# Global attention on one core: the values of two units back move ahead of the pair of trial scores

## What is computed

```python
def _L1_attn_ref(x, Wq, Wk, Wv, Wu, bu):      # b=2, t=1024, e=64, h=8
    scale = e ** (-0.25)
    q = (x @ Wq).reshape(b, t, h, e) * scale
    k = (x @ Wk).reshape(b, t, h, e) * scale
    v = (x @ Wv).reshape(b, t, h, e)
    dot = jnp.einsum('bqhe,bkhe->bhqk', q, k)
    att = jax.nn.softmax(dot, axis=-1)
    out = jnp.einsum('bhqk,bkhe->bqhe', att, v).reshape(b, t, h * e)
    return out @ Wu + bu
```

## Time and profile before

| | us |
|---|---|
| runs of the kernel before, three | 602.72, 610.61, 612.91 |
| their median | 610.61 |
| the profiled execution, device time | 602.83 |
| its span | 600.8 |
| PE busy in the span | 529.1 (88%) |
| DVE busy | 404.9 (67%) |
| ACT busy | 318.4 (53%) |
| global attention, from the first scores at 169.14 to about 476 | about 307 |

### The profile page before, as it was taken

The page is one execution under the profiler, slowest core; times in us unless marked ns, Lnnn a source line. Parts: engine busy times, 40 slices in busy tenths (PEclk is TensorE's granted clock), DMA queues, the critical chain, the costliest instruction groups (busy, mean ns, idle before and its releaser), DMA issues.

```text
span 600.8 us, 10365 instructions
## 1 busy us (share of the span) xinstructions
PE 529.1 (88%) x3951; PEld 255.0 (42%) x3952; DVE 404.9 (67%) x740; ACT 318.4 (53%) x584; POOL 49.8 (8%) x106
## 2 busy tenths in 40 slices
PE   6999998998599989999999999999999652799962
PEld 5554654554133335444334443344444320366721
DVE  5655557357886746876887686876662556898662
ACT  2735445565256575556656566666656332655440
POOL 7031232113110000000000010000000000000000
PEclk9999999699679999999999999999999957999975
DMA  5000000000000000000000000000000000000001
GB/s 112 5 1 2 2 2 2 0 2 2 0 1 1 1 1 1 2 0 1 1 1 1 1 2 1 1 9 1 1 1 1 2 3 15 1 1 1 1 0 35
DMA packets 9511, 3.28 MB, mean 5 GB/s; under 512 B 8820, under 2 KB 9079, under 8 KB 9463
## 3 DMA queue, kind: packets, MB, share of 16 engines
q1 hardware_dynamic: 8182, 2.61, 1.9%
q10 hardware_dynamic: 1281, 0.01, 0.1%
HBM read 2.09 MB, written 0.52 MB: 4 GB/s over the span
## 4 chain that ended last, share of the span: by engine, by line
PE 76%; DVE 10%; issue 8%; ACT 3%; POOL 1%; POOLq 0%; DVEq 0%; ACTq 0%
PE PS L786 18%; PE PS L763 18%; PE PS L747 5%; PE PS L667 4%; PE PS L681 4%; PE PS L694 3%; PE PS L518 2%; PE PS L490 2%; PE PS L502 2%; PE PS L802 2%; PE PS L708 2%; PE PS L989 2%; PE PS L564 2%; DVE most L1550 2%; PE PS L582 1%
## 5 line engine op out<-in xcount | busy, mean ns | idle before, releaser
L1189 ACT ACTIVATE PT<-PS 128x512 f32<-128x512 f32 x256 | 138.7, 593 | 78.7 <-PE PS L763 78.3
L1550 DVE TENSOR_REDUCE most<-PS 128x2 f32<-128x1024 f32 x128 | 154.4, 1221 | 33.9 <-PE PS L747 33.0
L763 PE MATMUL PS<-qrow,aS 128*64 128x512 f16 x1024 | 134.5, 383 | 1.8 <-ACT PT L1189 1.8
L786 PE MATMUL PS<-PT,V 128*64 128x512 f32 x512 | 134.4, 604 | 0.0
L763 PEld LDWEIGHTS PS<-qrow,aS 128*64 128x64 f16 x1024 | 58.8, 110 | 68.8 <-issue 22.9
L1145 ACT ACTIVATE prob<-sbias,negm 128x320 f32<-128x320 f32 (+1 forms) x64 | 34.3, 537 | 44.1 <-DVE negm L1596 43.9
L747 PE MATMUL PS<-aS,qrow 64*128 64x512 f16 x256 | 41.6, 397 | 7.0 <-DVE most L1550 6.2
L786 PEld LDWEIGHTS PS<-PT,V 128*64 128x64 f32 x512 | 32.0, 136 | 37.0 <-ACT PT L1189 17.9
L667 PE MATMUL PS<-ident 128*128 128x256 f16 x128 | 39.1, 306 | 7.5 <-DVE negm L1596 6.3
L1307 POOL TENSOR_TENSOR rstd<-var,minus_half 128x8 f32<-128x8 f32 (+1 forms) x9 | 13.5, 1505 | 343.5 <-DVE var L1414 343.5
L339 DVE COPY PT<-PS 128x384 f32<-128x384 f32 (+1 forms) x32 | 16.7, 523 | 29.4 <-PE PS L694 29.3
(11 more groups left out here) (192 smaller groups left out, 657.2 us busy)
## 6 DMA issues: line engine op xcount, KB each, us to landing
xall<-in_x_dram SPq DMA_DIRECT2D x2, 256.0 KB, 4.4
out_dram<-x SPq DMA_DIRECT2D x4, 128.0 KB, 2.1
w<-in_L_attn_Wq_dram SPq DMA_DIRECT2D x2, 128.0 KB, 2.6
w<-in_L_attn_Wk_dram SPq DMA_DIRECT2D x2, 128.0 KB, 2.7
w<-in_L_attn_Wv_dram SPq DMA_DIRECT2D x2, 128.0 KB, 2.7
fc<-in_L_conv_fc_w_dram SPq DMA_DIRECT2D x2, 64.0 KB, 2.7
wu<-in_L_attn_Wu_dram SPq DMA_DIRECT2D x2, 64.0 KB, 2.3
w1s<-in_L_ffn_ffn_w_dram SPq DMA_DIRECT2D x2, 64.0 KB, 2.1
```

What stands on the lines that cost most here:

```text
L763: mm = pe.matmul(PS[h0:h0 + C, lane, :], aS[:, part, k0 + h0:k0 + h0 + C], qG[:, lane, toks], start=(part == 0), stop=(part == 1))
L786: mm = pe.matmul(PS[cols, 6 + g % 2, :], V[:, img * NT + kt, cols], PT[:, g % 2, lane, kt, :], start=(kt == 0), stop=(kt == NT - 1))
L1189: act.activation(PT[:, g % 2, lane, phase, :], PS[:, lane, :], ACT.Exp).then_inc(c1["exped"], 1)
L1550: dve.tensor_reduce(most[:, g % 2, u // 2, u % 2, :], PS[:, b0:b0 + 2, :], AX.X, ALU.max, negate=True)\
```

## The change

Within a step of the global attention's loop the call of `glob_values(t - LAG_VAL)` stands ahead of the two calls of `try_scores` instead of behind them. Nothing else is changed: the same instructions, the same waits, the same banks.

```diff
                 if 0 <= t < UNITS:
                     scores(t)
+                if 0 <= t - LAG_VAL < UNITS:
+                    glob_values(t - LAG_VAL)
                 if 0 <= t + AHEAD < UNITS and (t + AHEAD) % 2 == 0:
                     try_scores(t + AHEAD)
                     try_scores(t + AHEAD + 1)
-                if 0 <= t - LAG_VAL < UNITS:
-                    glob_values(t - LAG_VAL)
                 if 1 <= g <= NG and phase in (Y_PHASE, Y_PHASE + 1):
                     head_outputs(g - 1, phase - Y_PHASE)
```

## The result

The changed kernel is slower. Its median was 618.34 us (609.08 to 620.44, 4 runs) beside 606.66 us for the kernel before, a ratio of 1.0174 (95% interval 1.0104 to 1.0244). The ratios leave out the executions that took over 1.5% more than the fastest of their kernel (here 620.44 and the profiled 619.74), so they are not the quotients of the medians. The two intervals only just meet, so the whole time alone gives the loss no better than "0.3 to 2.4%". The traces give it closer, once the stretch before the change is set aside.

A forecast was written before the change was run, and what follows sets the result against it. PE was taken as the bound of the global attention, with DVE setting the end at L816's wait; 9.1 - 1.3 + 0.7 = +8.5 us on 602.83 gave 611.3, or 619.1 from the median, put at 614, range 603 to 621.

The forecast's parts named there:

- The bound and the wait: Global attention: PE's list sets the time, except where L816 in phase 6 waits for DVE's second low query.
- Term 1: Phase 5: later trials delay DVE's reduction and low query, so L816 comes 0.70 us later; +9.1 us over 13 groups.
- Values followed by trials, 0.96: PE's blocks in changed steps: values to trials take 0.96 us start to start, bounds 0.86 and 1.01.
- Term 2: The 44 other changed steps: PE's blocks take 2.38 us instead of 2.41, -1.3 us in all.
- Term 3: L725 in phase 4 waits for L1666: 0 in quiet groups, +0.7 us in group 6 behind the key table.
- Sum: Whole kernel: 9.1 - 1.3 + 0.7 = +8.5 us.
- A: L816's wait is for something the trials don't move; 602.2 us, chance 0.12.
- B: PE's blocks fit better, values to trials 0.86 and trials to scores 0.43; 600 us, chance 0.06.
- C: L725 in phase 4 waits in all groups 1 to 12, adding 8.8 us; 620 us, chance 0.10.
- D: Longer PE gaps before L816 in groups 3 and 9 drop the granted clock; 616 us, chance 0.04.

The follow-up runs named there:

- e9: Kernel before, with one 0.69 us addition put on DVE's list ahead of phase 5's first reduction; ratio 1.0114, quiet group 18.95 us against 18.35.
- e2: Kernel before, with values ahead of trials in all phases but phase 5; quiet group 18.29 us against 18.35, no ratio given.
- e11: The changed kernel measured again on another chip with more rounds; 610.43 us beside 604.33 for the kernel before, ratio 1.0073.
- e10: Kernel before, with values first except in phase 5, second low query earlier, additions in phase 6, key table one step earlier; 597.43 us beside 604.33, ratio 0.9869.
- e7: Kernel before, with DVE's second low query right behind phase 5's first reduction and output additions moved to phase 6; ratio 0.9911, quiet group 18.07 us.

## Why the prediction was right, point by point

**The bound and the wait.** PE's list is the bound and L816's wait for the second low query is the one real wait of a quiet group: e9 lengthens that wait alone and pays in full.

**Term 1.** The trials stand 1.82 behind the scores, the reduction 2.25, L816 5.09, each as worked out. In groups 0 to 12 the way from the scores to L816 grew by 9.05 in all; the forecast was 13 x 0.70 = +9.1. Right, mechanism and size.

**Values followed by trials, 0.96.** Taken from L582's row. Measured 336.06 to 337.02: 0.96. Trials followed by scores 0.54 as well.

**Term 2.** Forecast -0.03 for a changed step, measured -0.06 for three steps in e2, so -0.02. Too small to matter. But I left out what follows the pair in some steps, and three of them count most. In steps 9, 15 and 17 a product L582 follows, and that one has the shape of the trials. These are the rows of step 15 in the changed kernel:

```profile
214.83 1.06 PE L763 MATMUL PS<-qrow,aS 128*64 128x512 f16 x8
215.69 1.05 PE L786 MATMUL PS<-PT,V 128*64 128x512 f32 x4
216.67 0.60 PE L747 MATMUL PS<-aS,qrow 64*128 64x512 f16 x4
217.12 1.02 PE L582 MATMUL PS<-prob,fc 64*128 64x512 f32 x2
218.06 1.05 PE L763 MATMUL PS<-qrow,aS 128*64 128x512 f16 x8
```

Scores to scores is 3.23 here and was 3.58 before (204.80 to 208.38). Trials to L582 is 0.45, where a change of shape behind trials makes it 0.54, and the values no longer stand between two changes of shape. Another 0.11 lies behind L582: 0.94 to the next scores here, 1.05 before (207.33 to 208.38), and why is open. This is the sum's mistake: three times -0.35, about -1 us. It is why group 2 (steps 15 and 17) was no longer than before, 23.87 against 23.86, in spite of its +0.70 at L816. Five more steps (7, 23, 39, 79 and 87) have L555, L591, L825 or L830 behind the pair; they became 0.14 to 0.24 shorter where the other steps of phase 7 became 0.05 shorter, which is another 0.6 us. The rule of the Trainium skill that I weighed (TensorEngine Tiling (Array Packing), Key Properties) says that a change of tiling mode drains the array. I had counted two changes in every step for either order. That holds where scores follow; with L582 behind the pair the old order has four changes up to the next scores and the new one two, at about 0.10 each. The rule agrees with these rows as far as those 0.20 of the 0.35 go; my count didn't.

**Term 3.** L725 held its place in quiet groups: its margin of 0.1 was enough. In group 6 the forecast was +0.7 on top; the group got 1.35 longer where quiet ones got 0.64. Right.

**Sum.** +8.5 forecast, +7.4 in e11's trace. The three L582 steps are about -1.0 of the difference and the five others -0.7; the remaining 36 steps of term 2 gave 0.02 each and not 0.03, +0.4. Terms 1 and 3 came out as forecast.

**The rivals.** A is out (L816 waits in all 13 groups). B is out: 0.96 and 0.54, not 0.86 and 0.43; a small part of it was true in the three steps. C is out: L725 waits in no quiet group. D is out: the granted clock is 1.00 in every window from 200 to 470 us, across gaps of up to 1.43 us in front of L816.

**The time.** 618.34 against a forecast of 614, within 603 to 621. That it lies so near to 614 is in part luck (609.6, where the runs of e11 gather, would have been in the range too): the change cost less than forecast, and three of the four runs had a mean granted clock of only 0.918 to 0.929, where the sum started from an execution at 0.942. I had put the time between two levels seen in three runs. The 17 runs of the kernel before beside e10 and e11 show something less tidy: eight lie at 602.3 to 603.1 with a mean granted clock of 0.942 to 0.945, three at 604.3 to 606.7, and six at 608.0 to 617.5 with 0.928 to 0.915. The sum was for the first kind; four of the changed kernel's twelve runs in e11 lie at 609.5 to 609.7, also at 0.945 to 0.948, 7.0 above. The forecast for an execution like the profiled one, 611.3, was 1.7 too high.

## What to carry to other kernels

Moving a block on the bounding engine costs nothing there and yet can cost a lot: ask for each consumer of the block what stands behind it in the consumer's in-order list, and whether the bounding engine waits for that later on. A mean busy share doesn't answer this; DVE was idle 30% of the time and had no slack at the one place. Where the result has several consumers with different slack, the order can be chosen per place (here: trials first in phase 5, values first elsewhere), and the dependent work that is urgent should stand ahead of what is not (the low query ahead of the additions): that was worth 0.9% (e7), and 1.3% with the order chosen per place and the key table a step earlier (e10). And count changes of the array's tile shape with the neighbour that really follows, not with the usual one.

## What the runs showed of the hardware that was not expected

With identical instructions the first 156 us ran at mean granted clocks of 0.90 to 0.98, and the first scores started anywhere from 168.1 to 177.4 us. That is more than the change is worth, and may be why two ratios of the same kernel are 1.0174 and 1.0073. What sets it was not tried and stays open, and the mean clock of the first 156 us doesn't tell it all: at 0.95 the first scores came at 168.14 in e2 and at 173.60 in e11.

A change of tile shape showed as 0.10 us at each border (scores to trials 0.97 instead of 0.86, values to trials 0.96), and was absent between two blocks of the same shape (trials to L582 0.45 against 0.54 to scores or outputs). The listed shape isn't all of it: L825 is a transpose listed as 128*64 like the values, and yet in the kernel before values behind trials took 1.01 until it (365.62 to 366.63), where 0.91 is usual until scores. Why a border costs time was not tested.
